# A graph kernel on one core: groups of tiles from a single tile on, shared masks in the prologue, another order of TensorE's work in the second edge stage, another split of the last stage

## What is computed

```python
def layer0(x, w, W, b, src, dst):               # graph convolution
    deg  = segment_sum(concat(w, ones), concat(dst, loop))
    dis  = where(deg > 0, rsqrt(deg), 0)
    msg  = (x @ W)[src_all] * (dis[src_all] * w_all * dis[dst_all])[:, None]
    return relu(segment_sum(msg, dst_all) + b)

def layer1(x, idx_i, idx_j, f_ij, rcut, r_ij, ...):   # idx_i = src, idx_j = dst
    xs, xv = x[:, :C] @ W_in2f_s, einsum(x[:, C:], W_in2f_v)
    sj, vj, Y = xs[idx_j], xv[idx_j], Y1 * r_ij / norm(r_ij)
    W   = ((softplus(f_ij @ Wf1 + bf1) - LOG2) @ Wf2 + bf2) * rcut
    m_s, m_v = products of (sj, vj, Y) by columns of W
    agg = segment_sum(concat(m_s, m_v), idx_i)
    S, V = agg[scalars] @ W1_s, einsum(agg[vectors], W1_v)
    return concat((softplus(S) - LOG2) @ W2_s, einsum(V, W2_v))

x = layernorm(x + layer0(x)); x = layernorm(x + layer1(x))
```

## Time and profile before

| what | us |
|---|---|
| median of three runs | 1092.49 (1091.48 to 1096.86) |
| profiled execution | 1102.86 |
| its span in the trace | 1101.1 |

### The profile page before, as it was taken

How to read it: one execution, slowest core, us unless ns; L and a number is a source line. 1 busy time by engine, 2 the same in 40 slices (tenths; PEclk the granted TensorE clock), 3 DMA queues, 4 the chain that set the end, 5 groups by cost and what they waited for, 6 DMA issues and landing times.

```text
span 1101.1 us, 17479 instructions
## 1 busy us (share of the span) xinstructions
PE 925.9 (84%) x4812; PEld 747.4 (68%) x4812; DVE 856.4 (78%) x2617; ACT 701.0 (64%) x1617; POOL 592.4 (54%) x679
## 2 busy tenths in 40 slices
PE   4989888989973999999999289999999999625553
PEld 4958777767753888888888168788788878514442
DVE  5888888868724788888879278888888888529997
ACT  0068877777761576676666346666666666439998
POOL 4017888788851566675666426677677765310000
PEclk9999999989995999999999699999999999955555
DMA  9979999999998599999997758999999998587996
GB/s 354 419 227 223 251 238 238 233 233 238 231 217 283 178 339 322 326 331 316 318 338 247 268 157 184 222 210 206 218 222 200 216 222 166 75 229 292 381 378 249
DMA packets 121553, 280.66 MB, mean 255 GB/s; under 512 B 13746, under 2 KB 38342, under 8 KB 121462
## 3 DMA queue, kind: packets, MB, share of 16 engines
q1 hardware_dynamic: 73590, 186.31, 46.8%
q0 software_dynamic: 35392, 82.86, 39.6%
q10 hardware_dynamic: 12480, 10.42, 2.9%
HBM read 132.44 MB, written 147.10 MB: 254 GB/s over the span
## 4 chain that ended last, share of the span: by engine, by line
PE 47%; ACT 8%; DMA 5%; issue 5%; DVE 3%; POOL 1%; SPq 0%; ACTq 0%; POOLq 0%; DVEq 0%
PE bank L1237 11%; PE bank L1284 6%; PE bank L1268 6%; PE bank L1241 5%; PE bank L1298 5%; PE bank L1296 3%; PE bank L1228 3%; PE bank L1262 2%; PE bank L1294 2%; PE bank L1269 2%; DMA edge_mem<-x 1%; ACT node_mem L799 1%; ACT node_mem L781 1%; ACT node_mem L791 1%; ACT edge_mem L770 1%
## 5 line engine op out<-in xcount | busy, mean ns | idle before, releaser
L532 POOL DMA_INDIRECT sum<-R_mem,sidx_all x79 | 128.6, 1628 | 93.9 <-DVE sidx_all L923 52.6
L589 POOL DMA_INDIRECT sum<-R_mem,l_sidx x79 | 130.3, 1650 | 52.9 <-ACT R_mem L727 18.2
L581 POOL DMA_INDIRECT G_mem<-x_d,dst_i x79 | 86.8, 1099 | 87.7 <-PE bank L1273 65.0
L1237 PE MATMUL bank<-G_hi 128*128 128x512 f32 x316 | 132.0, 418 | 0.0
L1237 PE MATMUL bank<-G_lo,G_hi 128*128 128x512 f32 x316 | 125.3, 396 | 0.0
L1153 PE MATMUL bank<-G_hi,M_mem 128*128 128x512 f32 x200 | 87.3, 437 | 9.9 <-ACT R_mem L630 9.9
L1314 PE MATMUL bank<-ident,node_mem 128*128 128x128 f32 x80 | 27.5, 447 | 71.4 <-DVE node_mem L1088 71.4
L1241 PE MATMUL bank<-G_hi,G_lo 128*128 128x512 f32 x316 | 85.5, 392 | 0.0
L1268 PE MATMUL bank<-edge_mem,Winv 128*128 128x512 f32 x158 | 82.6, 605 | 0.0
L1029 DVE SCALAR_TENSOR_TENSOR edge_mem<-edge_mem,Y,bank 128x128 f32<-128x128 f32 x237 | 71.3, 386 | 14.2 <-ACT edge_mem L733 14.2
L1153 PE MATMUL bank<-G_lo,M_mem 128*128 128x512 f32 x200 | 81.1, 406 | 0.0
(11 more groups left out here) (213 smaller groups left out, 2921.6 us busy)
## 6 DMA issues: line engine op xcount, KB each, us to landing
filt_d<-node_mem SPq DMA_DIRECT2D x40, 512.0 KB
node_mem<-filt_d SPq DMA_DIRECT2D x79, 256.0 KB
node_mem<-sum SPq DMA_DIRECT2D x39, 512.0 KB, 6.0
sum<-zeros SPq DMA_DIRECT2D x33, 512.0 KB
G_mem<-x SPq DMA_DIRECT2D x20, 512.0 KB, 6.6
x_d<-node_mem SPq DMA_DIRECT2D x20, 512.0 KB, 3.6
edge_mem<-x SPq DMA_DIRECT2D x19, 512.0 KB, 6.3
x_d<-R_mem SPq DMA_DIRECT2D x19, 512.0 KB, 3.7
```

The lines of the kernel that those rows point to most:

```text
L532: pool.indirect_dma_start(sum0, bass.IndirectOffsetOnAxis(ap=sidx[:, t:t + 1], axis=0), R[t % 8][:, :], None, compute_op=ALU.add).then_inc ...
L581: pool.indirect_dma_start(G3[t % 8][:, :], None, x1_d, bass.IndirectOffsetOnAxis(ap=dst_i[:, t:t + 1], axis=0)) \
L589: pool.indirect_dma_start(sum1, bass.IndirectOffsetOnAxis(ap=l1_sidx[:, t:t + 1], axis=0), R3[t % 8][:, :], None, compute_op=ALU.add).then ...
L1237: pe.matmul(bank[4 + a][:, :], zT_hi[a][:, c * P:(c + 1) * P], w[c][:, :], start=(c == 0 and w is W0h), stop=False)
```

## The change

- **Groups.** A group begins at `first(g) = max(3g - 2, 0)`: the first group holds one tile, all others three. Masks, rows of indices, counts, waits and scatters follow. The last tile's scatter takes the 16 rows that hold data.
- **edges1.** On TensorE Wins stands behind the scalar transpose, then come the second weights, and the sums stand last, for tile `s - 9` (it was `s - 10`). The values of the four waits are unchanged. The pipeline has one step less. ScalarE copies sums out by the new groups.
- **Turn-over.** POOL's first gather waits for x1's stores only; zeroing, scatter indices and sum stores are waited for ahead of the first scatter. The last pairs' `sum1` stores go behind the last `x1_d` store. The last two pairs' roots are made on VectorE (`n_root`), and the last tile is normalised there (`n_last`).
- **Prologue.** The degree loop is written out; from tile 14 on every second tile's `hot_lo` mask is made by ScalarE (two activations); the weights are combined inside the loop behind tile 50; the inverse root comes right behind the degree.
- **nodes1.** Softplus is `max(x, 0) + Ln(0.5 exp(-|x|) + 0.5)`, without L1070; POOL makes the tiny root (seven instructions) behind its scatters; ScalarE normalises half 0, VectorE half 1; 14 pairs are in flight, and stores wait for both halves.

```diff
+def by_act(t):
+    return t >= 14 and t % 2 == 0
+def first(g):
+    return max(3 * g - 2, 0)
 def tiles_of(g):
-    return min(3 * g + 3, TR) - 3 * g
+    return first(g + 1) - first(g)
+def place(t):
+    g = (t + 2) // 3
+    return g, t - first(g)
...
@@ SyncE, nodes0 @@
                     sp_.dma_start(layer_pair(x1_d, i, 0, D), in_pair(res2[i % 8], i, 0, D)).then_inc(n_st[i % 8], 16)
-                    sp_.dma_start(layer_pair(sum1, i, C, D), in_pair(res2[i % 8], i, C, D)).then_inc(n_st[i % 8], 16)
+                    for k in ((i,) if i < T2 - 2 else (i - 1, i) if i == T2 - 1 else ()):
+                        sp_.dma_start(layer_pair(sum1, k, C, D), in_pair(res2[k % 8], k, C, D)).then_inc(rows_st[k % 8], 16)
@@ GpSimd, ahead of the gathers @@
             for u in range(8):
-                pool.wait_ge(n_st[u], 32 * (T2 // 8))
-            pool.wait_ge(s_zero1, 16 * (T2 + 4))
-            pool.wait_ge(w_sidx, 2)
+                pool.wait_ge(n_st[u], 16 * (T2 // 8))
...
                     if r:
-                        pool.wait_ge(f_scat, 48 * r)
-                    for t in range(3 * r, min(3 * r + 3, TR)):
+                        pool.wait_ge(f_scat, 16 * first(r))
+                    else:
+                        pool.wait_ge(w_sidx, 2)
+                        pool.wait_ge(s_zero1, 16 * (T2 + 4))
+                        for u in range(8):
+                            pool.wait_ge(rows_st[u], SUM1)
+                    for t in range(first(r), first(r + 1)):
+                        n = min(N - t * P, P)
@@ GpSimd, behind the scatters @@
+            for t in range(T2):
+                a = t % 4
+                w, st = tiny4[a], Stage(g_rstd, t, K_ROOT)
+                pool.wait_ge(g_mv, K_MV4 * (t + 1))
+                st.mark(pool.tensor_scalar(w[:, 0, :], mv4[a][:, :, 1], EPS, None, ALU.add))
...
@@ ScalarE, degree loop @@
+            for t in range(T):
+                if by_act(t):
+                    tmp = spare[t // 2 % 2]
+                    act.wait_ge(s_deg_mm, t - 2)
+                    st.mark(act.activation(tmp, iota_f[:, :], ACT.Abs, bias=part[:, 0, t:t + 1], scale=-1.0))
+                    st.settle(act)
+                    st.mark(act.activation(hot_lo[t % 4], tmp, ACT.Relu, bias=1.0, scale=-1.0))
+                if t == MIDWAY:
+                    w_prep()
@@ VectorE, nodes1 @@
-                if live(s, 0, T2):
-                    dve.wait_ge(g_al[s % NA], 16 * (s // NA + 1))
-                    dve.tensor_scalar(sr[u][:, :, :], al[s % NA][:, :, 0:C], 0.0, -LOG2, ALU.max, ALU.add).then_inc(g_sr, 1)
...
+                if live(s, 7, T2):
+                    dve.wait_ge(g_rstd, K_ROOT * (t7 + 1))
+                    dve.tensor_scalar(al[b7][:, 1, :], al[b7][:, 1, :], tiny4[a7][:, 5, 1:2], tiny4[a7][:, 6, 1:2],
+                                      ALU.mult, ALU.add).then_inc(g_y1, 1)
@@ TensorE, edges1 @@
                     pe.matmul(bank[2][:, :], Winv[:, :], rawT[b][:, 0:512], start=True, stop=True)
-                    pe.matmul(bank[3][:, 0:P], Wins[:, :], rawT[b][:, 512:640], start=True, stop=True).then_inc(f_wv, 1)
                 if live(s, 4):
                     t, a = s - 4, (u - 4) % 8
                     wait(pe, f_us, t - 2)
                     pe.transpose(bank[5][:, 256:384], G3[a][:, 0:C], ident[:, :]).then_inc(f_tr, 1)
-                if live(s, 10):
-                    t = s - 10
...
+                if live(s, 5):
+                    pe.matmul(bank[3][:, 0:P], Wins[:, :], rawT[b][:, 512:640], start=True, stop=True).then_inc(f_wv, 1)
                 if live(s, 6):
                     t, b = s - 6, u % 2
...
                     ins.then_inc(f_o, 1)
-            for s in range(TR + 10):
+                if live(s, 9):
+                    t = s - 9
+                    g, j = place(t)
+                    last = t + 1 == first(g + 1)
+                    pe.wait_ge(f_lo, t + 1)
+                    pe.wait_ge(f_M, t + 1)
+                    for k in range(j + 1):
+                        if k == j and g and k < tiles_of(g - 1):
+                            pe.wait_ge(f_ev, first(g - 1) + k + 1)
...
+            for s in range(TR + 9):
```

More of the change, by code:

```diff
@@ L24 @@
 TAIL = TR - 4
+LATE = TR - 3
 NR = TR * P
@@ L63, in counted @@
 def counted(s):
-    return 3 * s + sum(tiles_of(extra(k)) for k in range(s) if extra(k))
+    return first(s) + sum(tiles_of(extra(k)) for k in range(s) if extra(k))
 def turn(t, slot, n):
@@ L478, in _ @@
             for s in range(4, TR):
-                g = s // 3
-                if s % 3 == 0 and g >= 4:
-                    sp_.wait_ge(f_M, 3 * (g - 3))
+                g, j = place(s)
+                if j == 0 and g >= 4:
+                    sp_.wait_ge(f_M, first(g - 3))
                     trow_in(g)
@@ L540, in nodes0 @@
             def nodes0(s, u):
-                if live(s, 9) and s % 2:
+                if live(s, 9, LATE) and s % 2:
                     g = (s - 9) // 2
@@ L680, in nodes0, with log @@
             def nodes0(s, u):
-                tail = live(s, 9) and s % 2
-                if tail:
-                    g = (s - 9) // 2
+                tail = live(s, 9, LATE) and s % 2
+                def log(g):
                     t, a = 2 * g, g % 4
@@ L686, in nodes0, with root @@
                     act.activation(tiny[a][:, 1, :], mv[a][:, :, 1], ACT.Ln, bias=eps_c[:, :]).then_inc(n_rs, 1)
+                def root(g):
+                    a = g % 4
+                    act.wait_ge(n_rs, 2 * g + 1)
+                    act.activation(tiny[a][:, 2, :], tiny[a][:, 1, :], ACT.Exp, scale=-0.5).then_inc(n_rs, 1)
+                if tail:
+                    log((s - 9) // 2)
                 if live(s, 2):
@@ L698, in nodes0 @@
                 if tail:
-                    act.wait_ge(n_rs, 2 * g + 1)
-                    act.activation(tiny[a][:, 2, :], tiny[a][:, 1, :], ACT.Exp, scale=-0.5).then_inc(n_rs, 1)
+                    root((s - 9) // 2)
+                if s == LATE + 10:
+                    for g in (T2 - 2, T2 - 1):
+                        log(g)
+                        root(g)
                 if live(s, 5, TAIL):
@@ L719, in _ @@
                 nodes0(s, s % 8)
+            for u in range(4, 8):
+                act.wait_ge(rows_st[u], SUM1)
             def edges1(s, u):
-                e = s - 11
+                e = s - 10
                 def sums_out(t):
                     act.wait_ge(f_mm, t + 1)
-                    wait(act, f_scat, 48 * (t // 3 - 1))
-                    act.copy(R3[t % 8][:, :], bank[sum_bank[t % 3]][:, :]).then_inc(f_ev, 1)
+                    if t >= 8:
+                        act.wait_ge(f_scat, 16 * first(place(t - 8)[0] + 1))
+                    act.copy(R3[t % 8][:, :], bank[sum_bank[place(t)[1]]][:, :]).then_inc(f_ev, 1)
                 if live(s, 7):
```

286 lines of the change are left out of this document (152 added, 134 removed).

## The result

| | median us | lowest to highest |
|---|---|---|
| before | 1092.2 | 1091.5 to 1096.9 |
| after | 1112.5 | 1109.5 to 1113.2 |

The account below looks back on a forecast made before the run. It took TensorE to bound layer 1's edge stage, and ScalarE and VectorE the last stage. The terms 33.7 - 5.1 - 3.1 - 1.8 - 6.9 = +16.8 on the median 1092.49 gave 1109 us, range 1095 to 1119.

Parts of the forecast that it names:

- A: Layer 1's edges, TensorE's order: sums put last no longer cover the wait for ScalarE's copy of the scalar transpose; +33.7 us.
- 316.6 and 350.3: Layer 1's edges: predicted us before and after the change, counted over the 79 steps that have second weights.
- B: Tail of scatters after layer 1's edges: two groups remain behind the last second weights instead of three; -5.1 us.
- the second 9.65: Tail of scatters: us from one group's first scatter to the next, counted again for the last group.
- C: Turn-over from layer 0's nodes: first gather waits for x1's stores alone, last roots move to VectorE; -3.1 us.
- D: Prologue: weights' preparation moves into the degree loop and VectorE's root comes earlier; -1.8 us.
- the -0.6: Prologue: us gained by moving the preparation of W1 into the degree loop.
- the -1.2: Prologue: us gained by VectorE's root before the first index rows, removing the 1.19 that L1198 waited at 61.04.
- E: Last stage: stores 2.65 us apart instead of 2.78 over 40 pairs, and one normalisation less at both ends; -6.9 us.
- (2): Prologue: writing out the degree loop removes VectorE's three stops, -7.7 us, total 1102, or 1095 with E better; chance 0.17.
- (3): Layer 1's edges: VectorE's L1038 holds the second weights, so three steps take 11.74 us; total -29, 1063; chance 0.11.
- (4): Layer 1's edges: TensorE's idle gaps lower the clock to 0.97, the stage grows by 10 us, total 1119; chance 0.17.

Follow-up runs that it names:

- the shared version: Against the changed kernel with its sums back between Wins and the second weights: ScalarE normalises both halves of every second last-stage pair; 1071.35 us against 1071.5.

## Why the prediction was right, step by step

**A, +33.7, measured +33.0: right, and by its mechanism.** The bare steps of the earlier trace rows gave the price of the uncovered wait, and the rounds came out at 13.46 (forecast 13.48). The same count for another order gave 14.14, measured 14.12. Its two totals, 316.6 and 350.3, are each some 5 above the measured 311.7 and 344.7, which cancels in the difference, and the idle time ahead of L1353 was 0.33, just under the 0.4 to 0.6 named as a sign. That ScalarE's copy and not VectorE's product ends the wait, against the name in the earlier trace rows, is shown by moving the transpose alone: the gap behind the transpose closes while the sums stay last, and L1351 starts 0.19 after the product L1123, before that ends.

**B, -5.1, measured -6.7.** The mechanism holds, two groups in place of three. The mis-sized term is the second 9.65: from the second group's first scatter to the load it was 990.24 - 982.73 = 7.5. Nearly all of the 2.1 is the last tile's scatter, for whose 16 rows I had taken only 0.3: it landed 3.73 after its issue, where the third scatter of a whole group took 5.3 to 5.7 (946.32 and 955.58 in the second trace of before).

**C, -3.1, measured -1.5 up to the second weights, -1.9 up to the gather.** The term "lands after 3.7 in the median" failed: the last x1 store took 5.33, about as long as the sum store's 5.21 in the earlier trace rows that had been waited for. So hardly anything came from the store's landing, and what came is the root and the last tile's normalisation on VectorE: from layer 0's last matmul to the last x1 store 7.2 us in place of 8.9. The gather's gain of 1.9 shrank by 0.4 on the way to the first second weights.

**D, -1.8, measured -1.1: near, but not by its terms.** Taking the stops at zero was right, and for the reason named as a doubt: they weren't in the other runs. Of the 10.4 between the profiled run and the median the stops were 7.7. TensorE's timeline of the prologue after:

```profile
11.63 19.23 PE L1198 MATMUL bank<-hot_hi,hot_mem 128*128 128x80 f32 x88
...
31.75 1.22 PE L1189 MATMUL bank<-W2v_r,W1vT 128*128 128x128 f32 x4 [0.46 <-ACT W1vT L641]
...
34.23 12.20 PE L1198 MATMUL bank<-hot_hi,hot_mem 128*128 128x80 f32 x56 [0.91 <-ACT hot_mem L654]
...
52.92 2.00 PE L1270 MATMUL bank<-dis,edge_mem 128*128 128x80 f32 x8
```

The loop runs on through the masks that ScalarE makes from tile 14; the weights' preparation stops its matmuls with 0.46 of waiting ahead of 1.22 of its own, and 0.91 of waiting stand behind it. Behind the loop TensorE waits 1.85 for ScalarE (L1209 at 49.85) and 0.83 for VectorE (L1264 at 51.01), in place of the 1.20 ahead of the lookup. The lookup's first matmuls stand at 52.92, against 52.73 in the second trace of before: nothing is gained up to there, so neither the -0.6 nor the -1.2 came. The 1.3 at the first sum of layer 0 (59.66 against 61.00) has another source: the two matmuls L1264 take 1.34 at 57.47, where the same two (L1192) took 2.07 at 57.28, and the lookup behind them 1.12 in place of 2.00. In after the granted clock rises from 0.50 to 1.00 (1.2 to 2.4 GHz) near 57.9; the trace of before lists 1.00 there with the longer matmuls, so the cause isn't shown. That D came out near its number is luck.

**E, -6.9, measured -4.2.** VectorE's step was right, 2.64 for 2.65, and so was the price of its new instruction, 0.46 for 0.43. The mis-sized terms are "over 40 pairs" (0.13 times 40 is also 5.2, not 5.3) and the two ends. Before, 32 of the 39 gaps between stores were 2.78, and the last seven, behind the last loads, 1.4 to 2.4 already. After, the first 32 gaps take 85.2 in place of 89.1, -3.9, since two of them are 3.00 and 2.92; the last seven give another -0.6. The first store follows the first load 0.4 sooner, and the end of the span follows the last store 0.7 later: -4.2 in all. The two late gaps stand in the run without POOL's root as well, 14 stores apart, both ahead of a store from `node_mem`, the fourteenth buffer; their cause wasn't tried.

**The rivals.** (2) falls with the loop written out: 0.9986. The mechanism that the Trainium skill ("Runtime: NRT & Kernel Launch", section "Instruction fetch mechanics") gave for it shows in no run here: a rolled and a written-out loop took the same time. (3) falls with the rounds of 13.46; its own number, 11.74 for bare TensorE work, is what the version with the sums back comes near to (11.85). (4) didn't happen: TensorE was busy for 92.5% of the stage and the granted clock stayed at 1.00 (2.4 GHz), so gaps of this size didn't lower it here. The 0.97 of layer 0's edges is a mean: in after the granted clock falls there to 0.50 (1.2 GHz) five times, for three to four us each. Four of the falls come behind pauses of TensorE of 3.51, 1.74, 2.36 and 2.62 us (from 61.31, 249.55, 276.01 and 300.42); the fifth, near 225, comes behind only 0.50, so pauses alone don't explain them all. Seven pauses of 1.4 in the same stage lowered nothing. By the rule of the Trainium skill ("SBUF — State Buffer", section "SBUF: two separate sides") E would have come out near 0. The run without POOL's root shows VectorE no faster without it, so here tiny instructions on POOL cost VectorE nothing, and the measurement decides; POOL's own took up to 0.37 for 0.19, which the rule allows for.

The sum came out low by 2.8 in the traces and by 3.5 in the medians, since C and E were taken too large and B too small. The gain that was there, 13.5 in B to E, needs A's order undone: with the sums back 17 to 20 us remain by the medians (1089.4 to 1072.95 and 1091.0 to 1071.5). By the traces it is 19.2 (1090.8 to 1071.6), which is the 13.5 and 25 rounds of 0.21.

## What to carry to other kernels

Work that stands between a producer and a wait on its consumer may be free; before it is moved, find a place where it is missing (the pipeline's first steps) and read the bare wait there. Where a row names a releaser that ended or began too close to tell, move one candidate by itself. A single profiled execution can hold a stall that other runs lack: when it stands apart from the median by as much as a term, take a second trace before comparing stages.

## What was not expected of the hardware

In one execution of the unchanged kernel VectorE stopped three times in the degree loop, 7.7 us in all; in a second one, and in the one of before with the sums behind the second weights, which has the same loop, it didn't. x1 stores landed after 3.7 us in the median of the earlier trace rows, and the last one of the kernel before after 4.2 and 4.4 in its two traces. In after, where two of them and two sum stores are issued close together (605.0 to 607.8), the last one took 5.33, and 5.3 to 5.6 in three more traces with this order. ScalarE's step without a second normalisation was 2.26 us with no idle time in the shared version, where the prediction had taken 2.1; the transfers ran at 400 GB/s there.
